# Linear attention with a mixture of experts: one tile between the stages of the expert loop, slot rows by DMA, twelve gathers ahead, final loads alternating

## The reference

```python
x = _layernorm(x + attn(x))          # 16 x 256 tokens of 256 numbers, 32 heads of linear attention with decay
x = _layernorm(x + ffn(x))
# ffn: 64 experts, 6 for each token, at most CAP = 48 tokens for each expert, taken in order
buf = zeros((E, CAP + 1, H)).at[se, slot].set(x[tok])[:, :CAP]
h = silu(einsum('ech,ehf->ecf', buf, w_gate)) * einsum('ech,ehf->ecf', buf, w_up)
out = einsum('ecf,efh->ech', h, w_down)
y = segment_sum(out[se, pos] * w, tok)
return y + silu(x @ ws_gate) * (x @ ws_up) @ ws_down   # routed experts + shared expert
```

## Time and profile before

| | |
|---|---|
| runs shown | 1346.82 us median of 3 (1346.51 to 1346.9) |
| the profiled execution | 1346.91 us |
| its span, first to last instruction | 1345.1 us |
| mean granted clock of PE | 0.993 |
| first records of the expert loop | 1212.63 us |
| last copy to `wo` ends | 1295.03 us |
| last scatter has landed | 1305.81 us |
| last ACT instruction ends | 1342.39 us |

### The profile page before, as it was taken

How to read it: one execution, slowest core, us unless ns; L and a number is a source line. 1 busy time by engine, 2 the same in 40 slices (tenths; PEclk the granted TensorE clock), 3 DMA queues, 4 the chain that set the end, 5 groups by cost and what they waited for, 6 DMA issues and landing times.

```text
span 1345.1 us, 39679 instructions
## 1 busy us (share of the span) xinstructions
PE 1302.3 (97%) x15324; PEld 1109.2 (82%) x15324; DVE 1022.5 (76%) x2324; ACT 923.4 (69%) x1738; POOL 477.4 (35%) x409
## 2 busy tenths in 40 slices
PE   7999999999999999999999999999999999988995
PEld 5788888888888888888888888888888888875464
DVE  6677878787878788787978787878878787873226
ACT  7667777777767777777777777777777777733435
POOL 0223243324233333424332423333342433234753
PEclk9999999999999999999999999999999999999998
DMA  7700000000000000000000000000000004485958
GB/s 290 274 2 10 28 9 13 23 2 27 9 27 10 27 9 27 10 27 9 21 15 2 27 9 27 18 27 17 27 18 27 17 19 135 127 253 134 231 100 329
DMA packets 47199, 81.11 MB, mean 60 GB/s; under 512 B 4465, under 2 KB 29137, under 8 KB 46161
## 3 DMA queue, kind: packets, MB, share of 16 engines
q1 hardware_dynamic: 37968, 65.58, 14.5%
q0 software_dynamic: 4608, 7.08, 3.0%
q10 hardware_dynamic: 4480, 6.29, 1.3%
HBM read 56.26 MB, written 22.68 MB: 59 GB/s over the span
## 4 chain that ended last, share of the span: by engine, by line
PE 88%; DVE 4%; DMA 3%; issue 2%; ACT 1%; POOL 1%; SPq 0%; another core or an unknown queue 0%; DVEq 0%; ACTq 0%; POOLq 0%
PE pA L570 25%; PE pB L570 24%; PE pO L669 12%; PE pC L655 10%; PE pS L632 10%; DMA sums<-sb_stage,sb_sidx 2%; PE pC L570 1%; DMA sb_W<-sums 1%; DVE sb_W L1213 1%; PE pS L874 1%; PE pB L854 1%; PE pS L854 1%; PE pS L882 1%; PE pC L694 1%; PE pS L753 1%
## 5 line engine op out<-in xcount | busy, mean ns | idle before, releaser
L1710 POOL TENSOR_TENSOR sb_vl<-sb_v,sb_vh 128x512 f16<-128x512 f32 x121 | 154.0, 1273 | 680.3 <-ACT sb_vh L975 680.3
L570 PE MATMUL pB<-sb_xh,sb_W 128*128 128x256 f16 x2048 | 350.2, 273 | 0.0
L1264 DVE TENSOR_TENSOR sb_S<-pS,sb_D 128x1024 f32<-128x1024 f32 x248 | 235.9, 952 | 120.6 <-PE pS L632 120.6
L983 ACT ACTIVATE sb_Shl<-sb_S 128x1024 f16<-128x1024 f32 x242 | 204.3, 844 | 110.6 <-DVE sb_S L1264 109.3
L570 PE MATMUL pB<-sb_xl,sb_W 128*128 128x256 f16 x1024 | 279.5, 273 | 0.0
L1270 DVE TENSOR_TENSOR sb_Shl<-sb_S,sb_Shl 128x1536 f16<-128x1536 f32 x121 | 225.3, 1862 | 10.5 <-ACT sb_Shl L983 10.4
L570 PEld LDWEIGHTS pB<-sb_xh,sb_W 128*128 128x128 f16 x2048 | 200.4, 99 | 23.1 <-DVE sb_W L1213 0.3
L570 PE MATMUL pA<-sb_xh,sb_W 128*128 128x256 f16 x1024 | 175.8, 274 | 10.4 <-DVE sb_W L1213 5.7
L570 PE MATMUL pA<-sb_W,sb_xh 128*128 128x256 f16 x1024 | 177.0, 275 | 3.4 <-ACT sb_qh L950 2.7
L669 PE MATMUL pO<-sb_Wo,sb_yh 128*128 128x256 f16 x1016 | 173.3, 273 | 0.0
L989 ACT ACTIVATE sb_gt<-pB 128x512 f32<-128x512 f32 x128 | 76.4, 597 | 140.5 <-PE pB L570 140.5
(11 more groups left out here) (319 smaller groups left out, 2690.5 us busy)
## 6 DMA issues: line engine op xcount, KB each, us to landing
sb_stage<-wprep SPq DMA_DIRECT2D x7, 1280.0 KB, 6.3
sb_W<-sums SPq DMA_DIRECT2D x16, 512.0 KB, 11.5
sb_W<-w_experts SPq DMA_DIRECT2D x17, 384.0 KB, 3.6
gather_rows<-sb_xr SPq DMA_DIRECT2D x16, 320.0 KB, 2.4
sb_xs<-xT SPq DMA_DIRECT2D x16, 256.0 KB, 2.9
sb_D<-decay SPq DMA_DIRECT2D x8, 512.0 KB, 7.3
sb_xn<-x SPq DMA_DIRECT2D x16, 256.0 KB, 3.0
sums<-sb_xr SPq DMA_DIRECT2D x16, 256.0 KB, 2.2
```

The lines of the kernel that those rows point to most:

```text
L570: last = nc.tensor.matmul(dst, a, m, start=(i == 0), stop=(i == len(terms) - 1), **kw)
L983: nc.scalar.activation(Sh[:, :, a:z_], S[:, :, a:z_], ACT.Copy).then_inc(s_Sh, 1)
L1264: nc.vector.tensor_tensor(scores_at(h)[:, :, a:z_], pS[:, :, a:z_], d[:, :, 0:z_ - a], ALU.mult).then_inc(s_Sm, 1)
L1710: nc.gpsimd.tensor_tensor(vl[q % 2][:, :, :], v32[:, :, :], vh[q % 2][:, :, :], ALU.subtract).then_inc(s_vl, 1)
```

## The change

- PE's order in iteration p becomes `gate_up(p)`, `down(p-1)`, `transpose_tokens(p+1)`, `transpose_inner(p)`, `merge(p-1)`; ACT's becomes `inner(p)`, `weighted(p-1)`, `evacuate(p+1)`, `evacuate_inner(p)`; DVE copies `wo` of tile p-1. The loop has 25 iterations where it had 27.
- `spread_ids` is left for the first two groups only. For the other 16 tiles SP writes `ids` to DRAM (2 DMAs of 8 and 4 KB), waits, and reads rows back over all partitions (8 DMAs of 128 KB).
- 12 gather buffers and 12 gathers ahead instead of 8. POOL starts `scatter(p)` before `gather(p+12)`.
- At the end the chunks go 0, 8, 1, 9, and so on. The first six are loaded in two halves, one for each region. POOL adds up chunks 1, 3, 5, 7 and finishes its shared products before the norms.

```diff
-XRING = 8
-AHEAD = 8
+XRING = 12
+AHEAD = 12
+ORDER = [c for i in range(8) for c in (i, 8 + i)]
+BY_POOL = (1, 3, 5, 7)
+SPLIT = 6
...
+            sp.wait_ge(s_find, FIND_LINKS * SEQS)
+            sp.dma_start(rows_main[:, :], ids[:, 0:BLOCK]).then_inc(s_ids_out, 16)
+            sp.dma_start(rows_rest[:, :], ids[:, BLOCK:CAP]).then_inc(s_ids_out, 16)
+            sp.wait_ge(s_ids_out, 16 * 2)
+            for run in ROW_RUNS:
+                src = main_runs[run] if run < TILES // KINDS else rest_runs[run - TILES // KINDS]
+                sp.dma_start(equal_pair[run], src.unsqueeze(0).broadcast_to([P, 2 * P])).then_inc(s_idb, 16)
...
-            for i in range(2):
-                sp.wait_ge(s_sc[i], 16 * (TILES // 2))
-            for c in range(FINALS):
+            for r in range(REGIONS):
+                sp.wait_ge(s_sc[r], 16 * (TILES // 2))
+                if r == 0:
+                    sp.wait_ge(s_md, TILES)
+                for c in ORDER[:SPLIT]:
+                    sp.dma_start(fin[c][:, r, :, :], regions[c][:, r, :, :]).then_inc(s_fl[c], 16)
+            for c in ORDER[SPLIT:]:
...
-            for p in range(TILES + 3):
+            for p in range(TILES + 1):
+                if p < TILES:
+                    gate_up(p)
+                if p >= 1:
+                    down(p - 1)
                 if p + 1 < TILES:
                     transpose_tokens(p + 1)
                 if p < TILES:
-                    gate_up(p)
-                n = p + 2
-                if n < TILES // EQB:
-                    pe.wait_ge(s_eq, (n if n > 2 else 1) * EQB)
-                    spread_ids(n)
-                if 1 <= p <= TILES:
-                    transpose_inner(p - 1)
-                if 2 <= p <= TILES + 1:
-                    down(p - 2)
-                if p >= 3:
-                    merge(p - 3)
+                    transpose_inner(p)
+                if p >= 1:
+                    merge(p - 1)
...
             for p in range(TILES):
+                scatter(p)
                 if p + AHEAD < TILES:
                     gather(p + AHEAD)
-                scatter(p)
-
-            unit_product(UNITS_AHEAD + 4)
-            unit_product(UNITS_AHEAD + 5)
-            for c in range(FINALS + 2):
-                if c >= 2:
-                    i = c - 2
+
+            for j in range(UNITS_AHEAD + 4, SEQS):
+                unit_product(j)
...
+            for n in range(FINALS + 2):
+                if n >= 2:
+                    i = n - 2
                     pool.wait_ge(s_fv, i + 1)
                     nc.gpsimd.tensor_tensor(frs[:, i % FACT, :], vv[:, :], mhalf[:, :], ALU.pow).then_inc(s_frs, 1)
-                    j = UNITS_AHEAD + 6 + i
-                    if j < SEQS:
-                        unit_product(j)
+                if n + 1 < FINALS and ORDER[n + 1] in BY_POOL:
+                    add_sums(ORDER[n + 1])
```

More of the change, by code:

```diff
@@ L254, in carve @@
             return flat[0:parts, at[-2]:at[-1]].rearrange("p (s n) -> p s n", s=bufs)
-        xg = carve(P, XRING, ROW)
+        in_stage = carve(P, XRING - 4, ROW)
+        xg = [in_stage[:, r, :] for r in range(XRING - 4)] + [a[:, 0:ROW] for a in (y32, sq)]
+        xg += [a[:, :, :].rearrange("p t n -> p (t n)")[:, 0:ROW] for a in (xn, z)]
         wo = carve(P, OUTBUF, HID)
@@ L264, in block_kernel, with equal_of @@
         mhs, mh = [a[:, :].bitcast(F32)[:, 0:2 * FF].rearrange("p (s n) -> p s n", s=2) for a in (yh, yl)]
-        equal = [floats(a)[:, s * P:(s + 1) * P] for a in (*kh, *kl, *vh, *vl) for s in range(2)]
-        equal += [a[:, s * P:(s + 1) * P] for a in (acc, xs) for s in range(4)]
-        assert len(equal) == TILES
+        equal_pair = [floats(a)[:, 0:2 * P] for a in (*kh, *kl, *vh, *vl)]
+        equal_pair += [a[:, s * 2 * P:(s + 1) * 2 * P] for a in (acc, xs) for s in range(2)]
+        def equal_of(t):
+            g, kind = t // KINDS, t % KINDS
+            pair, half = (g, kind) if kind < 2 else (TILES // KINDS + g // 2, g % 2)
+            return equal_pair[pair][:, half * P:(half + 1) * P]
+        equal = [equal_of(t) for t in range(TILES)]
         W32 = W[:, :].bitcast(F32)
@@ L416, in whole, with wait_sums, wait_whole @@
             return isinstance(h, int) and (h < WHOLE or h == LAST)
+        def wait_sums(eng, c):
+            eng.wait_ge(s_fl[c], 16 * (REGIONS if c in ORDER[:SPLIT] else 1))
+        def wait_whole(eng, c):
+            if c >= UNITS_AHEAD:
+                eng.wait_ge(s_fp, c - UNITS_AHEAD + 1)
+            elif c in BY_POOL:
+                eng.wait_ge(s_fpa, BY_POOL.index(c) + 1)
+            else:
+                eng.wait_ge(s_fadd, len([i for i in range(c + 1) if i not in BY_POOL]))
         def whole_rows(c, k):
@@ L1181, in _ @@
             evacuate(0)
-            for p in range(TILES + 2):
+            for p in range(TILES + 1):
+                if p < TILES:
+                    inner(p)
+                if p >= 1:
+                    weighted(p - 1)
                 if p + 1 < TILES:
@@ L1185, in _ @@
                 if p < TILES:
[L1186 to L1190, removed]
+                    evacuate_inner(p)
             for j in range(UNITS_AHEAD, SEQS):
                 unit_inner(j)
[L1194 to L1195 removed]
+            for n, c in enumerate(ORDER):
+                act.wait_ge(s_nm, n + 1)
                 for k in range(FIN):
                     last = nc.scalar.activation(fin[c][:, 1, k, :], whole_rows(c, k), ACT.Identity,
[L1198 removed]
+                                                scale=frs[:, n % FACT, k:k + 1], bias=nmr[:, n % FACT, k:k + 1])
                 last.then_inc(s_fo, 1)
[L1200 removed]
+                act.wait_ge(s_fo, n + 1)
                 act.dma_start(out_t[c], fin[c][:, 1, :, :]).then_inc(s_out, 16)
@@ L1627, in spread_equals @@
             def spread_equals(n):
-                dve.wait_ge(s_idr, n + 1)
+                if n < BY_PE:
+                    dve.wait_ge(s_idr, n + 1)
+                else:
+                    dve.wait_ge(s_idb, 16 * len(ROW_RUNS))
                 if n == 0:
@@ L1661, in _ @@
                 unit_product(j)
-            for c in range(FINALS + 2):
-                if c < UNITS_AHEAD:
-                    dve.wait_ge(s_fl[c], 16)
+            for n in range(FINALS + 2):
+                c = ORDER[n] if n < FINALS else None
+                if n < FINALS and c < UNITS_AHEAD and c not in BY_POOL:
+                    wait_sums(dve, c)
                     nc.vector.tensor_tensor(fin[c][:, 0, :, :], fin[c][:, 0, :, :], fin[c][:, 1, :, :], ALU.add).then_inc(s_fadd, 1)
-                if 1 <= c <= FINALS:
-                    i = c - 1
-                    dve.wait_ge(s_fst, c)
+                if 1 <= n <= FINALS:
+                    i = n - 1
+                    dve.wait_ge(s_fst, n)
                     if i >= FACT:
```

53 lines of the change are left out of this document (30 added, 23 removed).

## The result

The changed kernel took 1356.15 us, median of 5 runs (1354.83 to 1358.72), beside 1346.9 us for the kernel before (1346.51 to 1349.85, 5 runs): the ratio is 1.0065, with a 95% interval of 1.0051 to 1.008. The prediction said 1342.5. Two repeats on another chip, where the kernel before takes 1341.9 and 1341.7 us, gave 0.9974 (0.9964 to 0.9984) and 0.9977 (0.9967 to 0.9987). Both results hold, and what differs between those chips is the main finding.

A forecast was written before the change was run, and what follows sets the result against it. PE was taken to bound the expert loop, ACT the final normalisations. Last `wo` 1292.7 + 21.9 to first normalisation + 23.4 ACT + 2.7 store = 1340.7, + 1.8 around it = 1342.5 us; range 1338.5 to 1351.5.

The forecast's parts named there:

- the first rival: Expert loop: late ACT starts cost 12 tiles 0.3 to 0.67 us each, 4 to 8 us, so 1346 to 1350; chance 0.27.
- the forecast's own loop: From `gate_up(5)` to the end of the last copy to `wo`: 60.75 us.
- The start: Loop start: `inner(0)` stays 2.94 us behind `gate_up(0)`; `gate_up(5)` starts at 1231.95 instead of 1233.67, 1.7 us gained.
- The run of gathers holds the start: Loop start: four more early gathers delay the first wakes by 5 us, 1347.5; chance 0.13.
- Rows by DMA: Spreading slot rows: 4 us for 1 MB, ready 10 us ahead of use, hidden; otherwise at most 2 us.
- the case of both: Gathers holding the start together with half of the late-wakes rival: 1351 us, slower by a measurable amount.
- The argument from the Trainium skill: Expert loop: PE and ACT never wait for SBUF, so POOL's work would not cause late wakes; 1342.5 us would stand.
- The steady loop: Middle of the loop: 2.67, 3.32 and 3.10 us a tile, mean 3.03, against 2.82 of bare PE work.
- The last scatter: Behind the loop: starts 0.8 us behind the last `wo` and lands 3.83 later, near 1297.4 instead of 1305.8.
- The end: Behind the last `wo`: first normalisation after 21.9 us, then ACT bounds for 23.4, last store 2.7; 2.1 us gained.

The follow-up runs named there:

- the run on chip 10: Kernel before with one tile between stages, 12 gathers ahead and scatter ahead of gather, slot rows and end as before: 1355.75 us, ratio 1.0061.

## Why the prediction was wrong

**The step that failed** is the weighing of the first rival, *late wakes enter the chain*: "if PE itself ran late, then PE's records only hide a lag that a waiting PE does not build up". PE's completions do come late, and they come late while PE waits. The rows of before already showed them; the forecast entered 0.07 us for each wake-up and nothing for lateness. In its place the runs show 9.65 us in the loop (67.76 us against 58.11 without late ends). The rival's price was 4 to 8 us; against the forecast's own loop, which was 2.6 us too long, the measured one is 7.0 more and inside it.

**The start failed as a second step.** It was to shrink by 1.7 us and grew by 5.1 (26.08 for 20.96). *The run of gathers holds the start* had 0.13 and a price of 5 us. It came true in its price and in when the hold ends, not in how it was put: `inner(0)` was as late as before (2.47 us for 2.94), but the holds behind it went on, the last until 1224.20, 2.2 us behind the last early gather (1222.01), where in the kernel before DVE's wait ended at 1219.49, 2.15 behind the end of the eighth gather (1217.34), and ACT's at 1220.19. Rows by DMA are not needed for it: the version without them has a start of 26.85 us on chip 10. On chip 15 the start grows by 4.8 us for another reason, 3.7 of them the rows.

I treated the two rivals as nearly separate and gave only "half of the first rival" to the case of both, 1351. The sum that the measured pieces give: 1342.5 forecast, + 6.8 for the start (26.08 for 19.3), + 7.0 for the loop (67.76 for 60.75), + 0.3 for the end, - 0.5 because the loop began at 1212.16 and not at 1212.63, makes 1356.1, the measured 1356.15.

The argument from the Trainium skill ("SBUF — State Buffer", Who interferes with whom: PE and ACT never wait on anyone for SBUF) bore on the cause and not on whether there was lateness, and I let it count for the forecast. The late ends sit beside POOL's gathers and scatters on two chips and are absent beside the same ones on two others; no run here shows SBUF to be their cause.

**The other steps.**
- *The steady loop* was over-priced: 2.67, 3.32 and 3.10 us a tile; without late ends `gate_up` starts 2.53, 3.18 and 2.96 apart (2.89 on average for 3.03). The term at fault is `down`, 0.57 in before's stream and 0.43 when it follows `gate_up`. And before was not "PE's" alone: the earlier trace rows lack 1.45 us of 32, and twelve gathers, priced at nothing here, took 4.5 us out of the loop.
- *Rows by DMA*: "Hidden; if not, at most 2 us". DVE waited 3.28 us and the start lost 3.7. The 4 us for 1 MB became 10.6 beside the gathers. "A good 10 us ahead of their first use" was wrong as well: on chip 15 DVE wanted the rows at 1215.07, 7.4 us behind the first issue and 4.1 behind the last.
- *The start*: 2.94 us at `inner(0)` was kept as part of the program. It is a late end: on chip 15 the kernel before has 0.07 there, and its whole start takes 15.36 us for 20.96. That is the larger part of what that kernel loses between the chips; the end has another 1.6 us.
- *The last scatter* starts 0.75 us behind `wo` (0.8 forecast).
- *The end*: first normalisation 21.97 us behind `wo` (21.9), the whole 48.27 (48.0). But the new end has no part in the 2.1 us that were counted: the early scatters bring them. Behind early scatters the old end takes 46.2 to 46.8 us, where before has 48.40 on chip 15, and the new end gives 1.5 to 2 us of that back.
- Without late ends the forecast, 4.3 us faster, was near the 3.1 and 3.2 measured. That is luck in the main: errors cancelled, with the loop 2.6 better, the start 0.8 worse, and before itself 5 us faster.

**Shown**: the late ends go with the chip or its state and not with the program, and depth decides what lateness costs in the loop. **Open**: what makes them. In the changed kernel's loop they end at fixed places in POOL's indirect DMA instructions (1.4 to 1.5 us into a scatter, 0.3 behind a gather; in the kernel before also 0.7 to 0.8 into a scatter). There none behind the last gather (1272.4) is over 0.8 us, where earlier ones reach 1.6; but on chip 10, with lateness made by hand, one of 1.5 us comes 1.9 us behind the last gather. That is a correlation; a kernel without those DMAs was not run on such a chip, since only the last two runs met one. No version beat both kernels on every chip: order with twelve gathers is best where there are no late ends (0.9954) and loses where there are (1.0061). Twelve gathers in the old order kept their gain under lateness made by hand (0.998); on chip 10 it was not run.

## What to carry over

Depth between stages is paid in a drain at the end and returned as immunity: before it is taken away, sum how long behind its producer's recorded end each consumer between the two stages starts (idle time that a trace attributes to nobody, "remote" or "issue", is the sign), and charge it to the shallow version. Two rivals that rest on the same unexplained rows are one rival, to be priced together. A gain or loss below 1% that hangs on wake-ups should be measured on more than one chip, and its sensitivity can be tested anywhere by doing one instruction twice.

## What the runs showed of the hardware

- On chips 15 and 14, in twelve profiled runs (those with lateness made by hand left out), no ACT or DVE instruction that takes up PE's work in the loop started more than 0.16 us behind the later of PE's recorded end and its own engine's work before it; one exception, a last copy, has 0.54. Of the 120 hand-overs from PE (five a tile) 21 were over 0.5 us late in the kernel before on the chip of the result, 15 in the changed kernel there and 15 in the run on chip 10, and the longest had 2.9, 2.7 and 6.0 us. What the kernel before takes tells the sort of chip: 1341.6 to 1341.9 us, or 1346.9 to 1347.0.
- On both late chips the last long hold of the start ended 2.2 to 2.3 us behind POOL's last early gather.
- Of the 384 semaphore increments of the 24 gathers, the traces hold 368 to 384 in the sixteen runs on chips 15 and 14, and 143 to 198 in the four on the chip of the result and on chip 10.
- Lateness of 0.5 us made by hand in each of 24 tiles cost the loop 0.9 to 1.0 us with three tiles between the stages and 10.1 us with one.
- A row transfer of 128 KB to all partitions, the last of eight beside twelve gathers, took 7.35 us to land; all eight, 1 MB, took 10.6 us from the first issue.
